# A ternary feed-forward layer: float32 matmuls rewritten as bf16 matmuls in three parts, on one Trainium2 core

## What is computed

```python
def _ternary_linear(x, w):
    alpha = jnp.mean(jnp.abs(w))
    w_t = jnp.sign(w) * (jnp.abs(w) > 0.5 * alpha).astype(w.dtype)
    w_q = w + jax.lax.stop_gradient(w_t - w)
    d = x.shape[-1]
    rms = jnp.sqrt(jnp.sum(x * x, axis=-1, keepdims=True)) / jnp.sqrt(jnp.asarray(d, x.dtype))
    x_norm = x / (rms + EPS)
    return jnp.einsum('bsd,fd->bsf', x_norm, w_q)
h = jax.nn.gelu(_ternary_linear(x, w_up), approximate=False)
return _ternary_linear(h, w_down)
```

## Time and profile before

| | |
|---|---|
| three timed runs | 3507.61, 3488.12, 3496.45 us, median 3496.45 us |
| the profiled execution | 3478.68 us, its span 3476.5 us |
| first attention, start to about 1505 us | TensorE busy 96% in its middle |
| low-rank stage, about 1505 to 1845 us | |
| second attention, about 1845 to 2988 us | |
| ternary stage, about 2991 us to the end | TensorE busy 100%, VectorE 36% of a full batch |

### The profile page before, as it was taken

How to read it: one execution, slowest core, us unless ns; L and a number is a source line. 1 busy time by engine, 2 the same in 40 slices (tenths; PEclk the granted TensorE clock), 3 DMA queues, 4 the chain that set the end, 5 groups by cost and what they waited for, 6 DMA issues and landing times. The chain is left out here.

```text
span 3476.5 us, 78108 instructions
## 1 busy us (share of the span) xinstructions
PE 3129.8 (90%) x29924; PEld 2203.4 (63%) x29924; DVE 2289.0 (66%) x6197; ACT 1984.5 (57%) x3528; POOL 875.5 (25%) x1874
## 2 busy tenths in 40 slices
PE   3999999999999999988996888888888889799999
PEld 1677777777777777732333666766676667566666
DVE  2888888888888888844224666666666666333333
ACT  1888888888888888822331444444444445222222
POOL 0222222222222222216111222322222222233222
PEclk9999999999999999988997999999999999999999
DMA  5333333333333333210003443434343433000000
GB/s 152 60 56 58 58 58 58 58 59 58 58 58 58 55 55 56 39 41 0 0 0 69 79 76 61 80 61 80 64 76 64 77 63 51 1 19 19 19 19 25
DMA packets 109267, 182.65 MB, mean 53 GB/s; under 512 B 26336, under 2 KB 95712, under 8 KB 96416
## 3 DMA queue, kind: packets, MB, share of 16 engines
q1 hardware_dynamic: 105440, 176.87, 27.7%
q10 hardware_dynamic: 3456, 0.79, 0.2%
HBM read 116.51 MB, written 60.29 MB: 51 GB/s over the span
## 5 line engine op out<-in xcount | busy, mean ns | idle before, releaser
L1207 DVE TENSOR_REDUCE zeroed_max_cols<-bank 128x1 f32<-128x512 f32 (+3 forms) x1024 | 450.2, 481 | 251.6 <-PE bank L180 249.7
L1107 ACT ACTIVATE zeroed_prob<-bank 128x512 f32<-128x512 f32 x640 | 377.6, 597 | 326.6 <-PE bank L998 244.3
L636 DVE CUSTOM_DVE_ANT_0 ratio_scores<-ratio_scores 128x512 f32<-128x512 f32 (+3 forms) x1024 | 521.7, 537 | 22.1
L177 PE MATMUL bank<-ratio_k_stack,ratio_q_stack 102*128 102x512 bf16 (+7 forms) x2048 | 453.4, 303 | 66.4 <-ACT ratio_inv_root L506 46.4
L506 ACT ACTIVATE ratio_inv_root<-bank,eps_ratio 128x512 f32<-128x512 f32 x640 | 437.5, 684 | 111.6 <-PE bank L180 107.8
L627 DVE TENSOR_TENSOR ratio_scores<-bank,ratio_inv_root 128x512 f32<-128x512 f32 x640 | 437.8, 684 | 62.1 <-PE bank L177 54.9
L425 PE MATMUL bank<-const_f_sb,ratio_scores 128*128 128x128 f32 x2560 | 451.5, 274 | 1.1 <-ACT ratio_prob L515 0.4
L508 ACT ACTIVATE ratio_inv_root<-ratio_inv_root 128x512 f32<-128x512 f32 x640 | 404.0, 631 | 20.3
L180 PE MATMUL bank<-const_b_sb 128*128 128x128 bf16 x2048 | 393.4, 224 | 0.0
L515 ACT ACTIVATE ratio_prob<-bank 128x512 f32<-128x512 f32 x640 | 370.5, 579 | 6.0 <-PE bank L431 5.8
L425 PEld LDWEIGHTS bank<-const_f_sb,ratio_scores 128*128 128x128 f32 x2560 | 301.3, 141 | 59.1 <-DVE ratio_max_cols L636 2.2
(11 more groups left out here) (176 smaller groups left out, 5613.9 us busy)
## 6 DMA issues: line engine op xcount, KB each, us to landing
ratio_q_stack<-ratio_parts_q SPq DMA_DIRECT2D x192, 128.0 KB
ratio_k_stack<-ratio_parts_k SPq DMA_DIRECT2D x192, 128.0 KB
zeroed_q_stack<-zeroed_parts_q SPq DMA_DIRECT2D x192, 128.0 KB, 4.6
zeroed_k_stack<-zeroed_parts_k SPq DMA_DIRECT2D x192, 128.0 KB, 7.2
ratio_parts_q<-ratio_parts SPq DMA_DIRECT2D x96, 128.0 KB
ratio_parts_k<-ratio_parts SPq DMA_DIRECT2D x96, 128.0 KB
zeroed_parts_q<-zeroed_parts SPq DMA_DIRECT2D x96, 128.0 KB
zeroed_parts_k<-zeroed_parts SPq DMA_DIRECT2D x96, 128.0 KB
```

Of the source, the lines that this page charges most:

```text
L177: i = e.matmul(bank[:, off:off + w], qs[0:rows, s, hh, ib * P:(ib + 1) * P], ks[0:rows, s, hh, 0:w], start=(k == 0), stop=mask is None, sk ...
L636: i = e.tensor_tensor_reduce(seg, seg, seg, 1.0, 0.0, ALU.mult, ALU.max, mx[:, pair % M_BUFS, c:c + 1])
L1107: e.activation(prob[:, n % FOLD_PROBS, 0:wd], exp_banks[n % 2][:, 0:wd], ACT.Exp, scale=0.25).then_inc(s["prob"])
L1207: i = e.tensor_reduce(mx[:, pair % FOLDS, c:c + 1], bank[:, off:off + (ib + 1) * P], AX_X, ALU.max)
```

## The change

- The ternary weights are kept in bf16, which holds -1, 0 and 1 exactly. The two rounding steps of GpSimd (L1675, L1678, twice each) are gone.
- x and h are each split in three bf16 parts, high, middle and low. `up` is 6 matmuls of 512 columns and `down` 12 of 256 columns, all bf16.
- Gelu writes back into its bank. ScalarE then copies the bank to the high part and squares the bank (`high_part`, `square`). VectorE subtracts (`split_rest`), casts to the middle part (`split_mid`) and subtracts again (`split_low`), the last of these one slot later. VectorE no longer squares.
- There are three banks for `up`, and `down` comes three slots later (`T_LAG = 3`). `row_sums` shares `prep_bank` with the transposes.
- The rows of x are normalised by GpSimd, ahead of its additions at f = 0 and 2. The transposes are at f = 1 and 4, ScalarE copies their high part, and VectorE makes the rest (`split_x`, at f = 2 and 5). `row_sums` and the root are at f = 5, and `finish` is one tile a slot from f = 6 on.

The core of the diff:

```diff
-TERNARY_SEMS = """up_loaded down_loaded w_abs w_abs_row w_abs_sum threshold neg_threshold w_above w_below w_t
-    w_t_less w_q"""
+TERNARY_SEMS = "up_loaded down_loaded w_abs w_abs_row neg_threshold w_above w_below w_t"
...
-        sb = lambda n, s: ctx.enter_context(net.nc.sbuf_tensor(f"ternary_{n}", s, F32))
+        sb = lambda n, s: ctx.enter_context(net.nc.sbuf_tensor(f"ternary_{n}", s, BF16))
...
-                if i == 3:
-                    q.wait_ge(s["w_t"], k + 1)
-                    e.tensor_tensor(pos, pos, w, ALU.subtract).then_inc(s["w_t_less"])
-                if i == 4:
-                    q.wait_ge(s["w_t_less"], k + 1)
-                    e.tensor_tensor(pos, pos, w, ALU.add).then_inc(s["w_q"])
...
+T_LAG = 3
+H_BANKS = 3
+T_XN_AT, T_TURN_AT, T_SPLIT_AT, T_SUMS_AT, T_SCALE_AT, T_FINISH_AT = (0, 2), (1, 4), (2, 5), 5, 5, 6
...
             def turn_x(b, pair):
                 q.wait_ge(s["xn"], 2 * b + pair + 1)
-                q.wait_ge(s["xnT"], 2 * b + pair)
+                q.wait_ge(s["x_rest"], 2 * b + pair)
+                if pair == 0:
+                    q.wait_ge(s["h_rms"], b - 2)
...
             def up(n):
-                q.wait_ge(s["xnT"], 2 * b + 2)
-                q.wait_ge(s["gelu"], n - 1)
+                q.wait_ge(s["x_lo"], 2 * b + 2)
+                q.wait_ge(s["h_rest"], n - H_BANKS + 1)
                 for c in range(2):
-                    i = e.matmul(h_banks[n % 2][:, :], ternary.up[:, c, f * P:(f + 1) * P], xnT[:, b % 2, c, :],
-                                 start=(c == 0), stop=(c == 1))
+                    for part in range(3):
+                        i = e.matmul(h_banks[n % H_BANKS][:, :], ternary.up[:, c, f * P:(f + 1) * P], x_parts[:, b % 2, part, c, :],
+                                     start=(c == 0 and part == 0), stop=(c == 1 and part == 2))
...
             def down(n):
-                q.wait_ge(s["gelu"], n + 1)
-                q.wait_ge(s["x_added"], b - 1)
+                q.wait_ge(s["h_lo"], n + 1)
+                q.wait_ge(s["x_added"], added(b - 2) if b >= 2 else 0)
...
             def row_sums(b):
                 q.wait_ge(s["h_summed"], (b + 1) * (FC - 1))
                 q.wait_ge(s["h_rms"], b)
+                q.wait_ge(s["x_rest"], min(2 * (b + 3), 2 * B))
...
+            def gelu(n):
+                q.wait_ge(s["up"], n + 1)
+                e.activation(h_banks[n % H_BANKS][:, :], h_banks[n % H_BANKS][:, :], ACT.Gelu).then_inc(s["gelu"])
...
+            def split_x(b, pair):
+                at = 2 * b + pair
+                part = lambda k: x_parts[:, b % 2, k, :, pair * 256:(pair + 1) * 256]
+                q.wait_ge(s["x_hi"], at + 1)
+                q.wait_ge(s["up"], (b - 1) * FC)
+                q.wait_ge(s["x_lo"], at)
+                e.tensor_tensor(x_rest[:, :, :], prep_bank[:, :].rearrange("p (c t) -> p c t", c=2), part(0),
+                                ALU.subtract).then_inc(s["x_rest"])
...
+            def split_rest(n):
+                q.wait_ge(s["h_hi"], n + 1)
+                q.wait_ge(s["h_squared"], n + 1)
+                q.wait_ge(s["h_lo"], n - 1)
+                e.tensor_tensor(h_rest[:, n % 2, :], h_banks[n % H_BANKS][:, :], h_parts[:, n % H_BUFS, 0, :],
+                                ALU.subtract).then_inc(s["h_rest"])
+
+            def split_mid(n):
+                q.wait_ge(s["h_rest"], n + 1)
+                q.wait_ge(s["down"], n - H_BUFS + 1)
+                e.tensor_copy(h_parts[:, n % H_BUFS, 1, :], h_rest[:, n % 2, :]).then_inc(s["h_mid"])
+
+            def split_low(n):
+                q.wait_ge(s["h_mid"], n + 1)
+                e.tensor_tensor(h_parts[:, n % H_BUFS, 2, :], h_rest[:, n % 2, :], h_parts[:, n % H_BUFS, 1, :],
+                                ALU.subtract).then_inc(s["h_lo"])
...
-            for n in range(n_slots + FC):
+            for n in range(n_slots + 2 * FC):
                 b, f = divmod(n, FC)
                 if n < n_slots:
-                    square(n)
-                if b + 1 < B:
-                    if f in (1, 2):
-                        keep_x(b + 1, f - 1)
-                    if f < 2:
-                        normal(b + 1, f)
-                if b and f == 3:
-                    finish(b - 1)
+                    split_rest(n)
+                if 0 <= n - 1 < n_slots:
+                    split_low(n - 1)
+                if n < n_slots:
+                    split_mid(n)
+                if b + 1 < B and f in T_SPLIT_AT:
+                    split_x(b + 1, T_SPLIT_AT.index(f))
+                if 0 < b <= B and f == T_SCALE_AT:
+                    hidden_scale(b - 1)
```

More of the change, by code:

```diff
@@ L1727, in ternary_feed_forward @@
         sb = lambda n, s, d=F32: ctx.enter_context(nc.sbuf_tensor(f"ternary_{n}", s, d))
-        s = semaphores(nc, ctx, "ternary", """std scale rms xn turned xnT up gelu h_squared h_summed down h_rows h_rms
-            h_rms_eps h_scale x_added stored""")
+        s = semaphores(nc, ctx, "ternary", """std scale rms xn turned x_hi x_rest x_mid x_lo up gelu h_hi h_squared h_rest h_mid h_lo
+            h_summed down h_rows h_rms h_rms_eps h_scale x_added stored""")
+        added = lambda b: T * (b + 1)
         scale = sb("x_scale", [P, B * T])
@@ L1762, in down @@
                 banks = down_banks[2 * (b % 2):2 * (b % 2) + 2]
-                q.wait_ge(s["gelu"], n + 1)
-                q.wait_ge(s["x_added"], b - 1)
+                q.wait_ge(s["h_lo"], n + 1)
+                q.wait_ge(s["x_added"], added(b - 2) if b >= 2 else 0)
                 for t in range(T):
-                    i = e.matmul(banks[t // 2][:, (t % 2) * D:(t % 2 + 1) * D], hidden[:, n % H_BUFS, t * P:(t + 1) * P],
-                                 ternary.down[:, f, :], start=(f == 0 and t % 2 == 0), stop=(f == FC - 1), skip_group_check=True)
+                    for part in range(3):
+                        i = e.matmul(banks[t // 2][:, (t % 2) * D:(t % 2 + 1) * D],
+                                     h_parts[:, n % H_BUFS, part, t * P:(t + 1) * P], ternary.down[:, f, :],
+                                     start=(f == 0 and t % 2 == 0 and part == 0), stop=(f == FC - 1 and part == 2),
+                                     skip_group_check=True)
                 i.then_inc(s["down"])
@@ L1797, in act @@
                 if n < n_slots:
-                    q.wait_ge(s["up"], n + 1)
-                    q.wait_ge(s["down"], n - H_BUFS + 1)
-                    q.wait_ge(s["h_squared"], n - H_BUFS + 1)
-                    e.activation(hidden[:, n % H_BUFS, :], h_banks[n % 2][:, :], ACT.Gelu).then_inc(s["gelu"])
-                if b and f == 3:
+                    gelu(n)
+                    high_part(n)
+                    square(n)
+                if b + 1 < B and f in T_TURN_AT:
+                    keep_x(b + 1, T_TURN_AT.index(f))
@@ L1803, in act @@
+                if b and f == T_SCALE_AT:
                     q.wait_ge(s["h_rows"], b)
-                    q.wait_ge(s["x_added"], b - 2)
-                    e.activation(hs[:, (b - 1) % 2, :], post_bank[:, 0:T], ACT.Sqrt, scale=1.0 / F).then_inc(s["h_rms"])
+                    q.wait_ge(s["x_added"], added(b - 3) if b >= 3 else 0)
+                    e.activation(hs[:, (b - 1) % 2, :], prep_bank[:, 0:T], ACT.Sqrt, scale=1.0 / F).then_inc(s["h_rms"])
         def dve(q):
             e = q.e
-            def normal(b, pair):
-                q.wait_ge(s["scale"], 2)
-                q.wait_ge(s["turned"], 2 * b + pair)
-                for tt in range(2):
-                    t = b * T + 2 * pair + tt
-                    i = e.tensor_scalar(xn[:, tt, :], net.x[:, t, :], net.mean_var[:, t, 0:1], scale[:, t:t + 1],
-                                        ALU.subtract, ALU.mult)
-                i.then_inc(s["xn"])
```

98 lines of the change are left out of this document (60 added, 38 removed).

## The result

| | before | after |
|---|---|---|
| median of 20 timed runs | 3496.2 us (3475.9 to 3508.8) | 3505.8 us (3496.4 to 3521.4) |
| profiled execution | 3478.68 us | 3516.39 us |
| low-rank stage in the profile | 331.3 us | 330.4 us |
| second attention in the profile | 1150.1 us | 1175.1 us |
| ternary stage in the profile | 485.3 us | 498.3 us |

The account below looks back on a forecast made before the run. The ternary stage was taken as bound by TensorE. Middle batches -18, first and last -13, stage ends +5, low-rank stage -1.5 gave -28 us: 3451 us profiled, 3468 us timed; forecast's own range 3452 to 3485, overall 3430 to 3497 us.

Parts of the forecast that it names:

- the wait of the row sums: Ternary stage: TensorE stands 3.6 us behind `down` until VectorE has made `x_rest` of the second pair, 14 times.
- the clock behind it: TensorE's granted clock falls after that wait: 2.0 us lost a batch, with 0 and 3.5 kept as bounds.
- the short waits: No term in the batch sum; VectorE's total of 22 to 24 us was put under the batch's 28 us.
- TensorE's work: Ternary batch: eight slots of 2.58 us plus 1.7 us for transposes and row sums, 22.4 us.
- GpSimd's normalisation: Ternary stage: each normalisation of 256 columns takes 0.7 to 0.9 us, at the rate of L1666.
- The start: Start of the ternary stage: first `up` comes 3.2 us later (2 to 5) through normalisations and the split of x.
- The end: End of the ternary stage: about 6.5 us from the last `up`, 1.3 us more than before.
- the slot of 2.60 us: Ternary stage: `up` and `down` at 1.29 us each make a slot of 2.58 us, 0.87 us less.
- that rival: Ternary stage: 18 weight loads a slot do not hide, slot 4.4 us, +120 us, 3617 us; chance 0.03.
- the 1.5 us forecast: Low-rank stage: dropping two of GpSimd's roundings, each done twice, gains 1.5 us, between nothing and 4 us.
- the clock takes more: Ternary stage: clock loses 3.5 us or the wait is over 4 us, batch 29.5 us, 3490 us; chance 0.17.
- The rival of a VectorE that sets the pace: Ternary stage: no wait; VectorE with GpSimd in its way sets the batch at 23.7 us, 3409 us; chance 0.08.

Follow-up runs that it names:

- experiment 10: Changed kernel with GpSimd's addition of each slot also waiting for that slot's `split_mid`; 3482.9 us, ternary stage 491.2 us.
- Experiment 2: Changed kernel with 12 unused bf16 matmuls of 512 columns put ahead of the waiting row sums; 3484.3 us, ternary stage 461.3 us.
- Experiment 7: Changed kernel with GpSimd's additions of the squares on 1 column of 512, a pricing run only; 3453.2 us, ternary stage 449.6 us.
- experiment 3: Changed kernel with the four normalisations of a batch moved from GpSimd back to VectorE; ternary stage 494.9 us.
- version 6: Changed kernel with second transpose at f = 3, its split at 4, row sums and root at 6, VectorE normalising; median 3421.9 us, ratio to before 0.9785.
- experiment 8: version 6 with GpSimd's additions on 1 column of 512, a pricing run only; 3392.0 us, batch 23.00 us.
- experiments 9: version 6 with GpSimd's addition of each slot also waiting for that slot's `split_mid`; median 3418.4 us, ratio to before 0.9797.
- 11: Changed kernel with VectorE normalising and row sums, root and `finish` at f = 7; 3484.3 us, ternary stage 488.7 us.
- 12: Changed kernel with VectorE normalising, row sums and root at f = 7, two `finish` a slot at f = 7 and 0; median 3427.6 us, ratio 0.9816.

## Why the prediction was wrong

It forecast 28 us less; the median is 10 us longer, and the two changed stages of the profile are 12 us longer. The mechanism was the one named, the wait of the row sums on L1863 and the clock behind it, in 14 batches. It was the sum that failed, by 2.7 us a batch, in two terms above all: the clock, 1.0 us too small, and the short waits, 1.2 us that were put at nothing.

| a batch | predicted | measured |
|---|---|---|
| TensorE's work | 22.4 | 22.6 |
| the wait of the row sums | 3.6 | 3.9, start to start; 3.68 in the bracket |
| the clock behind it | 2.0 | 3.0 |
| waits before `down` and the transposes | none | 1.2 |
| together | 28.0 | 30.7 |

- **The clock** is the first step that failed: "I take 2.0 us, nearest the first, and keep 0 and 3.5." The rows that it came from the earlier trace rows had losses of 1.5 and 2.9 us. These are close to the two sizes that the runs showed, 1.7 and 3.0 to 3.2 us, and experiment 10 has both behind one length of gap. A value between them was a mean of two cases. The larger came in 13 of the 14 gaps. Experiment 2 shows that the whole 3.0 us hangs on the gap.
- **The wait** was sized right, in part by luck. The working had TensorE's `down` end 1.3 us and `x_rest` 4.9 us after the end of `up(5)`; they ended 2.1 and 5.8 us after it (3220.85 and 3224.56 against 3218.73, TensorE's ends taken by its steps of 1.29 and 1.31 us), so two misses of 0.8 to 0.9 us cancelled. The working had `split_low` held up beside GpSimd in slot 5. In fact that addition held up the cast of slot 4, and VectorE was 1.7 us late when slot 5 began. Experiment 7 confirms the split: 2.9 us by order, 0.8 us by GpSimd.
- **The short waits** are the second step that failed: the sum has nothing for them. TensorE idled 0.65 us before `down(2)`, ended by a `split_low` of 1.63 us beside an addition, and 0.23 us before one transpose, ended by GpSimd's L1938 (0.8 and 0.4 us from start to start). I had put VectorE's total under the batch's length and asked no more; a total that fits says nothing on a chain that is late in one slot.
- **GpSimd's normalisation** was forecast at 0.7 to 0.9 us from the rate of L1666. It took 1.21 us at the least and 1.72 us in the median. By experiment 3 this hardly mattered in the batch (0.3 us).
- **The start**: the first `up` came 5.1 us later than before, not 3.2. With VectorE normalising (experiment 3) it is still 3.6 us later, and GpSimd's share is 1.5 us, no more than the working had for it (4 x 0.4); so most of the miss lies in the other steps up to the first `up`; which of them is not shown.
- **The end**: from the last `up` to the row sums 8.0 us instead of 5.2, +2.8 where +1.3 was forecast; two of the last four `down` waited 0.85 and 1.52 us.
- **Right**: the slot of 2.60 us, so weight loads are hidden and that rival is out; three ScalarE passes of 0.58 to 0.60 us. Whether the low-rank stage gained the 1.5 us forecast is open: its 0.9 us less is inside what its unchanged code varied by.

14 x (30.6 - 28.0) = 36 us of the miss of some 40 are the batches' (30.6 is the mean of the first 13 periods), and the rest start and end. The rival "the clock takes more" had the mechanism and a batch of 29.5 us; with the 1.2 us of short waits added it is what happened. It was given 0.17, and its clock of 3.5 us was nearer than the forecast's.

The rival of a VectorE that sets the pace is true only once the long wait is gone: in version 6 VectorE is busy 98% of a batch, of which 4.2 us are GpSimd's doing (experiment 8). The Trainium skill, "SBUF — State Buffer", section "Who interferes with whom", says that VectorE and GpSimd share a pair of SBUF ports, which one instruction holds to its end, and that VectorE needs it for two SBUF inputs or in its fast modes. The rows agree: L1884, with two SBUF inputs, and the cast L1880 were drawn out from 0.68 and 0.41 to 1.63 and 1.48 us; L1863 and L1874, with one input in PSUM, were at 674 to 693 ns in all their 160 instances.

## What to carry to other kernels

Where a change makes TensorE cheaper, ask first which instruction of its stream waits for something written late in another engine's same slot: here one slot of distance was worth 69 us of stage, five times what the whole change had cost. Price a gap of TensorE of 3 us or more at its length and the larger of the clock losses that the trace shows, not at a value between them. And move by timeline, not by totals: experiments 9, 11 and 12 each took away a wait and found the next one at an instruction that had been early enough until then.
